# One core's fused block (attention and a mixture of experts): one routing group, token products moved between gate and up products, the last base in the late blocks, later combines in the tail

## What is computed

```
h = layernorm(x) * (1 + ca) + sa
x = x + ga * attention(h)
h = layernorm(x) * (1 + cb) + sb
aff = sigmoid(h @ wa)                       # 16 experts
topk_p, topk_i = top_k(aff, 2)              # shares, normalised to sum 1
routed = sum over the 2 chosen experts of share * w2(gelu(g(h)) * w1(h))
shared = sum over 2 shared experts of the same form, on every token
x = x + gb * (h + shared + routed)
```

## Time and profile before

| what | value |
|---|---|
| median of three executions | 1434.72 us |
| profiled execution | 1445.19 us, its span 1443.4 us |
| mean granted TensorE clock | 0.974 of full |
| busy: PE, DVE, ACT, POOL | 95%, 60%, 47%, 27% of the span |
| stage after attention | from 980.5 us to the end |

### The profile page before, as it was taken

One profiled execution on the slowest core, in us unless ns is written; L12 is line 12 of the kernel. 1 busy time (PEld: TensorE's weight loads), 2 busy tenths in 40 slices (PEclk: granted clock), 3 DMA queues, 4 the chain that ended last, 5 costly groups with the idle time before them and its releaser, 6 DMA issues. The chain is left out here.

```text
span 1443.4 us, 23277 instructions
## 1 busy us (share of the span) xinstructions
PE 1371.2 (95%) x7104; PEld 1150.2 (80%) x7104; DVE 859.9 (60%) x1776; ACT 673.5 (47%) x1554; POOL 383.9 (27%) x345
## 2 busy tenths in 40 slices
PE   6999998999999999999999999998997999999968
PEld 3666777888888888888888888886775888878756
DVE  5787754666666665666866666556565544434366
ACT  3343426666666566665766666643221332223221
POOL 0343462000003180030910307300052322322360
PEclk9999999999999999999999999999988999999979
DMA  9999868956686688776899767947343888886481
GB/s 293 363 390 349 299 252 290 358 195 226 201 308 232 194 271 290 271 261 222 295 372 334 224 203 247 333 170 272 135 166 137 300 327 314 335 306 230 131 270 44
DMA packets 160042, 375.59 MB, mean 260 GB/s; under 512 B 23144, under 2 KB 80556, under 8 KB 147680
## 3 DMA queue, kind: packets, MB, share of 16 engines
q1 hardware_dynamic: 144432, 314.34, 62.0%
q0 software_dynamic: 15536, 60.30, 11.7%
HBM read 245.84 MB, written 128.22 MB: 259 GB/s over the span
## 5 line engine op out<-in xcount | busy, mean ns | idle before, releaser
L1155 ACT ACTIVATE a_pr<-a_pr,a_stat 128x128 f32<-128x128 f32 (+3 forms) x256 | 142.0, 556 | 114.2 <-DVE a_stat L1226 114.1
L1326 PEld LDWEIGHTS a_psY<-a_pT,a_cv 128*128 128x128 f32 x768 | 124.2, 189 | 15.7 <-issue 2.1
L1226 DVE CUSTOM_DVE_ANT_0 a_pr<-a_psS,f_mask 128x128 f32<-128x128 f32 (+3 forms) x256 | 114.6, 486 | 32.5 <-PE a_psS L1314 32.1
L1326 PE MATMUL a_psY<-a_pT,a_cv 128*128 128x512 f32 (+3 forms) x768 | 130.3, 319 | 1.9 <-DVE a_pT L1245 1.9
L1161 ACT ACTIVATE a_pr<-a_pr,a_stat 128x128 f32<-128x128 f32 (+3 forms) x256 | 122.2, 548 | 0.0
L1171 ACT ACTIVATE a_oT<-a_psY 128x512 fp32r<-128x512 f32 x64 | 38.2, 596 | 150.6 <-PE a_psY L1326 150.6
L1256 DVE TENSOR_TENSOR n_acc<-a_psZ,n_acc 128x512 f32<-128x512 f32 x125 | 86.4, 691 | 36.2 <-PE a_psZ L104 33.9
L1240 DVE TENSOR_TENSOR a_oT<-a_psY,a_oT 128x512 fp32r<-128x512 f32 x64 | 44.2, 691 | 102.6 <-ACT a_oT L1171 102.6
L102 PE MATMUL a_psX<-a_hT,a_wqk 128*128 128x512 f32 (+1 forms) x256 | 100.4, 392 | 0.6 <-DVEq L1216 0.6
L103 PE MATMUL a_psX<-a_hT,a_wqk 128*128 128x512 f32 (+1 forms) x256 | 100.4, 392 | 0.0
L104 PE MATMUL a_psX<-a_hT,a_wqk 128*128 128x512 f32 (+1 forms) x256 | 100.1, 391 | 0.0
(11 more groups left out here) (357 smaller groups left out, 3499.3 us busy)
## 6 DMA issues: line engine op xcount, KB each, us to landing
w1s_d<-a_ws SPq DMA_DIRECT2D x72, 512.0 KB, 2.9
a_wqk<-wqk_d SPq DMA_DIRECT2D x64, 512.0 KB, 4.7
a_mh<-mhl_d SPq DMA_DIRECT2D x32, 1024.0 KB
s_ring<-w1s_d SPq DMA_DIRECT2D x16, 2048.0 KB, 9.1
w2s_d<-a_ws SPq DMA_DIRECT2D x72, 256.0 KB, 3.4
qpe_d<-p_qs SPq DMA_DIRECT2D x16, 1024.0 KB, 5.1
a_rw<-in_L_ffn_rw SPq DMA_DIRECT2D x128, 128.0 KB, 3.5
a_qpe<-qpe_d SPq DMA_DIRECT2D x64, 256.0 KB, 2.7
```

Source lines behind the costliest of these rows:

```text
L1155: nc.scalar.activation(pr[i], pr[i], ACT.Exp, bias=nmax[:, i:i + 1], scale=-1.0, accum_out=rsum[:, i:i + 1]).then_inc(ex, 1)
L1226: nc.vector.tensor_tensor_reduce(out=pr[i], in0=score[i][:, 0:w], in1=mask[:, S - w:S], scale=-1.0, scalar=3e38, op0=ALU.add, op1=ALU.min, ...
L1326: m = nc.tensor.matmul(psY[:, q0:S], cv[:, j, cs], pT[:, ps, o:o + w], start=n == 0, stop=n == 11)
```

## The change

One group of tiles does the routing. The transposes of batch 3 move ahead of batch 0's second products, DVE's second modulation of h moves ahead of `times(0, 2)` for that. The token products move into `first_(1, 3)`: 2 after each of the four feature chunks of the gate products, 4 after each of the up products, and the last 8 into `first_two(1)`, between its two tiles. POOL makes 18 of the 32 marking matrices and DVE 14, each signalled by itself. `tables` moves ahead of `times(1, 2)`, `shares` into block 1. `bs` is laid over the last 8 marking matrices, is not cleared any more (the one-hot rows are zero where it is not written), and its DVE part moves behind `update(1, 0)`. `last_base` moves from blocks 0 to 3 into blocks 40 to 43, and SP's wait for it behind the load of batch 2's h. AHEAD goes from 3 to 2, and the table of combines changes. The diff, cut to its core:

```diff
-            bs = sb("s_bs", [P, 2, 2 * F], F32R, own)
+        bs = hx[:, 1, 2:TB].bitcast(F32R)
...
-        AHEAD = 3
+        AHEAD = 2
...
-        tiles_m = {LAST: [[], [0], [1, 2], [3, 4]], 2: [[14], [15], [], []]}
+        tiles_m = {LAST: [[], [], [0], [1, 2]], 2: [[11], [12], [13], [14]]}
...
                 sp.dma_start(late.rearrange("p c s n -> p (c s n)").bitcast(F32),
                              K.h2T_d.rearrange("p c s n -> p (c s n)")).then_inc(late_in, 16)
+                sp.wait_ge(base3, 1)
+                for b in range(B):
+                    sp.dma_start(gb4[:, b], K.mod_d[b:b + 1, 5 * D:6 * D].broadcast_to([P, D])).then_inc(g4_in, 16)
...
-                for b in range(LAST):
-                    spots_of(b)
+                for n in range(NP):
+                    nc.gpsimd.tensor_scalar(spots[:, n], line, low[:, n // NT, n % NT:n % NT + 1], ids[:, n % NT:n % NT + 1],
+                                            ALU.is_equal, ALU.mult).then_inc(spots_ok, 1)
...
-                act.wait_ge(bs_zero, 1)
+                act.wait_ge(taken, 1)
...
-                for i in range(5, 14):
+                for i in range(3, 11):
                     scaled(i)
...
+                N.last_modulated(dve, h3, 1, ALU.add, 4, h3_ok)
+                constants_()
                 times(0, 2)
                 y_low(0, 2)
-                N.last_modulated(dve, h3, 1, ALU.add, 4, h3_ok)
-                constants_()
+                h_low(LAST, 0)
+                h_low(LAST, 1)
+                h_low(LAST, 2)
                 times(0, 3)
+                h_low(LAST, 3)
                 y_low(0, 3)
...
                 update(0, 0)
                 update(0, 1)
+                best(m1, oh1)
+                best(m2, oh2)
                 update(0, 2)
                 update(0, 3)
-                ranked(0, early)
                 times(1, 0)
                 y_low(1, 0)
-                best(m1, oh1, 1, end_)
-                best(m2, oh2, 1, end_)
+                ranked()
+                counts()
+                blocks_of()
                 times(1, 1)
                 y_low(1, 1)
-                ranked(1, end_)
-                counts()
-                blocks_of()
-                last_spots()
+                last_spots(range(NP, 25))
+                tables()
                 times(1, 2)
                 y_low(1, 2)
-                shares()
-                tables()
+                last_spots(range(25, TOP * NT))
                 times(1, 3)
                 y_low(1, 3)
                 tokens()
-                v.memset(bs[:, :, :].bitcast(U32), 0).then_inc(bs_zero, 1)
...
-                    if t == 0:
+                    if t == 1:
                         dve.wait_ge(bs_hi, 1)
...
-                    if not past(j, u, XS):
+                    if isinstance(j, int) and j == 0 and u == 1:
+                        shares()
+                    if isinstance(j, int) and j == JL - 1:
                         if u == 0:
                             dve.wait_ge(gb_in, 16 * 3)
                             dve.wait_ge(h3_out, 16)
                         N.last_base(ch, h3, gbr, u)
...
-                for i in (5, 6, 7):
+                for i in range(3, TB + TB):
                     combine([i])
                 combine([8], True)
+                finish([8])
                 combine([9], True)
-                finish([8, 9])
+                finish([9])
                 combine([10], True)
                 finish([10])
-                combine([11], True)
-                finish([11])
-                combine([12, 13], True)
                 for m in range(NU):
                     times(2, m)
                     y_low(2, m)
                     combine(tiles_m[2][m], True)
+                    if m == 0:
+                        finish([11])
+                combine([15], True)
...
                 first_(0, 2, 1, up)
+                pe.wait_ge(h3_ok, 1)
+                x_trans(LAST, 0)
                 by_token(0)
                 router(1)
+                x_trans(LAST, 1)
                 first_(0, 3, 0, gate)
                 by_token(1)
                 router(2)
+                x_trans(LAST, 2)
                 first_(0, 3, 1, up)
+                x_trans(LAST, 3)
                 first_two(0, lambda: by_token(2))
-                pe.wait_ge(h3_ok, 1)
-                x_trans(LAST, 0)
-                order(0, early)
+                router(LAST)
                 second(0, 2)
-                x_trans(LAST, 1)
+                by_token(LAST)
                 second(0, 3)
-                x_trans(LAST, 2)
                 first_(1, 0, 0, gate)
-                x_trans(LAST, 3)
+                order()
                 first_(1, 0, 1, up)
...
+                        if o < NP:
+                            pe.wait_ge(spots_ok, o + 1)
+                        else:
+                            pe.wait_ge(last_ok, o - NP + 1)
...
+                first_(1, NU - 1, 0, gate, lambda c: take(2))
+                first_(1, NU - 1, 1, up, lambda c: take(4))
+
+                def last_takes():
+                    take(8)
+                    taking[1].then_inc(taken, 1)
...
+                first_two(1, last_takes)
```

More of the change, by code:

```diff
@@ L1387, in stage_ffn @@
     NK = NBLK + 1
+    NP = 18
     JL = NBLK // XS
@@ L1734, in _ @@
                 logits(0)
+                h_high(LAST, 0)
                 y_high(0, 2)
                 logits(1)
+                h_high(LAST, 1)
                 gelu(0, 3)
                 logits(2)
+                h_high(LAST, 2)
+                h_high(LAST, 3)
                 y_high(0, 3)
-                affinity(0, early)
-                for c in range(DC):
-                    h_high(LAST, c)
-                gelu(1, 0)
                 logits(LAST)
-                y_high(1, 0)
-                affinity(1, end_)
-                for m in range(1, NU):
+                affinity()
+                for m in range(NU):
                     gelu(1, m)
@@ L1901, in tokens, with tables @@
                     v.tensor_copy(token[:, :], pl[:, 0:NK]).then_inc(token_ok, 1)
[L1903 to L1909 removed]
+                def tables():
                     ch.after(v.tensor_copy(lead[:, :], first[:, :]))
@@ L2121, in by_token, with first_ @@
                     m.then_inc(lg_t, 1)
-                def first_(b, m, a, done):
+                def first_(b, m, a, done, between=None):
                     n = place_of[b] * NU + m
@@ L2137, in first_ @@
                         r = nc.tensor.matmul(pg[:, m % 2, a], w1[:, e, c, 1, o], h[:, c, 0], start=False, stop=c == DC - 1)
+                        if between is not None:
+                            between(c)
                     r.then_inc(done, 1)
@@ L2247, in _ @@
                 first_(1, 0, 1, up)
[L2248 to L2255 removed]
+                for m in range(1, NU - 1):
                     first_(1, m, 0, gate)
                     first_(1, m, 1, up)
[L2259 to L2270 removed]
+                taking = [0, None]
@@ new lines, in take @@
+                def take(n):
+                    for _ in range(n):
+                        o = taking[0]
+                        if o % NT == 0:
+                            pe.wait_ge(takes_ok, o // NT + 1)
+                        if o < NP:
+                            pe.wait_ge(spots_ok, o + 1)
+                        else:
+                            pe.wait_ge(last_ok, o - NP + 1)
+                        taking[1] = nc.tensor.matmul(pl[:, 0:NK], spots[:, o], takes[:, o], start=o == 0, stop=o == TOP * NT - 1)
+                        taking[0] += 1
```

151 lines of the change are left out of this document (46 added, 105 removed).

## The result

| what | before | changed |
|---|---|---|
| median of four executions (lowest to highest) | 1434.55 us (1433.55 to 1438.87) | 1422.47 us (1421.50 to 1426.09) |
| profiled execution, its span | 1445.19, 1443.4 us | 1421.54, 1419.7 us |
| transposes of block 1's product | 1108.40 | 1097.98 |
| transposes of the last block's rows | 1340.98 | 1328.97 |
| from there to the end ("the tail") | 102.4 us | 90.7 us |

The ratio is 0.9915, with a 95% interval of 0.9887 to 0.9942: 12 us, or 0.85%, faster. The forecast was 1410, 24.6 us faster, so about half of it came. Against the *profiled* execution of before, though, the changed kernel's profiled execution is 23.7 us shorter, and the forecast sum was 25. Both facts need an explanation.

What follows compares the result with a forecast made beforehand. It took TensorE's waits and half clock on either side of the blocks as the bound. Front 18 plus tail 7 is 25 us, taken from 1434.7 for 1410 us, range 1398 to 1424.

Steps and rivals of the forecast that it cites:

- the front's 18 us: Routing through block 1 and just behind: block 1's transposes 17.9 us earlier, 2.1 after them, less 2 for slow clock.
- the tail's 7 us: Behind the last block: 3.5 + 2.5 - 0.5 - 1.5 + 3 = 7 us gained.
- The base and its wait: Ahead of block 1's transposes: moving `last_base` late removes PE's 5.9 us wait and slow clock; base's share 8 us.
- Bounds: 0 and 10 us of extra time. I take 2: Token products among batch 1's up products: the slow clock still costs 2 us, in a shorter stretch.
- Products 16 and 17 wait for its last matrices, 2 us in all: Batch 1's up products catch up with POOL's marking matrices; PE waits 2 us, bounds 0 and 5.
- I take 0.3: Gathers of rows ahead of block 1: PE waits 0.3 us for their landing, bounds 0 and 4 us.
- the half clock through the token products: Rival: TensorE's clock stays down through the token products, costing 8 us more, 1418 us; chance 0.18.
- The load chain: Blocks: SP's expert loads start earlier, cost 0. Rival: they do not, front's gain is lost, 1428 us; chance 0.04.
- The 3 us for unnamed waits: Tail: fewer gathers in flight shrink DVE's 5.6 and ACT's 3.8 us unnamed waits by 3 us, bounds 0 and 9.
- the 2.5 us for `times(LAST, 3)`: Tail: one combine less ahead lets it start between 1.8 and 4.5 us earlier; 2.5 us in the sum.
- unmoved unnamed waits: Rival in the tail: DVE's 5.6 and ACT's 3.8 us stay whole, tail gives 4 us, 1413 us; no separate chance given.
- The layout: Rival in the front: gathers or bias rows still wait for the token list, only the base's 8 us, 1420; chance 0.05.

Runs made afterwards that it cites:

- experiment 3: The kernel before with only `last_base` moved into blocks 40 to 43, its gate rows loaded behind it: 1426.6 us, ratio 0.992.
- experiment 1: The changed kernel with the old tail (AHEAD = 3 and the table of combines of before): 1423.8 us, ratio 0.9913.
- experiment 4: The changed kernel with `last_base` moved back into blocks 0 to 3: 1431.3 us, ratio 0.9968.
- experiment 7: The changed kernel with POOL making 12 marking matrices instead of 18 and `tables` moved behind `y_low(1, 3)`: 1416.6 us, ratio 0.9801.
- experiment 16: The changed kernel with POOL making 12 marking matrices, `tables` behind `y_low(1, 3)` and expert 1's w1 load issued later: 1413.4 us, ratio 0.9841.
- experiment 9: The kernel before, unchanged, run and profiled again on another chip: 1441.9 us, ratio 1.0008.
- experiment 10: The kernel before with AHEAD = 2 and nothing else: 1436.9 us, ratio 0.9988.
- experiment 14: The changed kernel with AHEAD = 4 and nothing else: 1422.5 us, ratio 0.9911.
- experiment 2: The kernel before with only the new tail (AHEAD = 2 and the new table of combines): 1433.4 us, ratio 0.9976.
- experiment 11: The changed kernel with the old tail (AHEAD = 3, old table of combines), run again on another chip: 1431.1 us, ratio 0.9943.
- experiment 12: The changed kernel, unchanged, run again on another chip: 1422.8 us, ratio 0.9883.
- experiment 13: The changed kernel with AHEAD = 3 and nothing else: 1422.0 us, ratio 0.9907.
- experiment 5: The changed kernel with POOL making 12 marking matrices instead of 18 and DVE 20: 1420.5 us, ratio 0.9817.
- experiment 6: The changed kernel with `tables` moved from ahead of `times(1, 2)` to behind `y_low(1, 3)`: 1424.1 us, ratio 0.9847.

## Why the prediction was right or wrong

Two steps failed: the front's 18 us, of which some 10.5 came, and the tail's 7 us, carried unchanged from the profiled execution to the median, where some 2 came.

**The base and its wait: right.** Block 1's 5.9 us wait and the slow clock behind it, 8 us of the 18, came as worked out; put in alone it gave 8.8 us (experiment 3), and taken out it left the kernel 7.5 us above experiment 1 on the same chip, which has the old tail besides (experiment 4). Of the ends forecast in the routing several were within a microsecond or so: the 0.4 us wait for the ranks (0.40), POOL's start (1051.3, measured 1050.3), the last matrix (1066.8, measured 1067.9; as this execution was 1.5 us ahead at 1004, the last is really 2.6 us late). PE does not wait for the bias rows.

**The routing and its token products: the term that was mis-sized.** Block 1's transposes were forecast at 1090.5 and stand at 1097.98, though this execution was 1.5 us ahead at 1004, before the two lists part. The front and the blocks gave 12.0 us instead of 18, and 10.5 without that head start. The parts of the shortfall:
- "Bounds: 0 and 10 us of extra time. I take 2": the slow clock cost about 4.5 us, by the busy time in it. The reason given, that 512-column products follow at once, held for its end and not for its start. I charged the waits for POOL as lost time only; the half clock came with them too, for with 1.0 us of waits instead of 2.7 it is 1.00 throughout (experiments 7 and 16). The 12.7 us at half clock from which I started were no fixed cost of the kernel before either: in experiments 9 and 10 its token products run at full clock.
- "Products 16 and 17 wait for its last matrices, 2 us in all": 2.7 us in six pieces, since a matrix took 0.98 us and not 0.86. The upper bound had the reason in it ("1.1 us beside a busier DVE").
- "I take 0.3" for the gathers: 1.3 and 1.1 us. The bounds were 0 and 4, and I took the end at which nothing happens, although I had named the three MB of weights in flight. That the load is what made the gather late is not shown, for other executions of this front have waits for rows from 0 to 1.6 us. The 1.1 us may hold the 0.7 us of turn-around at `update(1, 0)` that the sum had: in experiments 4 and 14, without a wait for rows, PE waits 0.7 us there for DVE.
These make 5.3 us, or 4.6 without that 0.7; some 2 more between the prediction's walk and the trace are small and not taken apart. Seen from the rival list, the half clock through the token products (1418, chance 0.18) was the nearer case, but half of its reason was wrong: experiment 7 has the same small products at full clock. Of the signs named for being wrong one appeared, a wait for gathered rows.

**The blocks: right to a microsecond, in the sum.** The load chain moved with block 2 (SP's wait fell from 18.0 to 10.8 us) and the later base cost nothing that PE saw. The waits for two experts grew by 2.3 us; the half clock behind such a wait, some 4 us of it from 1287 on in the kernel before, fell away.

**The tail: 7 us, and the step from the profile to the median, which is where it failed.** One combine and one finish less ahead of `times(2, 0)` is 3.5 us; PE's wait there fell from 9.5 to 10.6 us (experiments 3, 1 and 9) to 6.4 to 7.6, and the tail from 94.0 to 97.2 us without a stall to 90.7 to 93.0: right. The other terms are read from `times(LAST, 3)` and `times(2, 0)` in the changed kernel and then in experiment 1, the same front with the old tail and no stall:

```profile
1363.94 0.75 DVE L1817 SCALAR_TENSOR_TENSOR s_y<-s_pg,s_bT,s_y 128x512 f32<-128x512 f32 x1 [1.17 <-PE s_pg L2124]
...
1391.31 0.75 DVE L1817 SCALAR_TENSOR_TENSOR s_y<-s_pg,s_bT,s_y 128x512 f32<-128x512 f32 x1
...
1363.18 0.74 DVE L1816 SCALAR_TENSOR_TENSOR s_y<-s_pg,s_bT,s_y 128x512 f32<-128x512 f32 x1
...
1393.64 0.74 DVE L1816 SCALAR_TENSOR_TENSOR s_y<-s_pg,s_bT,s_y 128x512 f32<-128x512 f32 x1
```

Counted from the last block's rows, `times(LAST, 3)` starts 35.0 us on instead of 35.4: 0.4 us earlier, where I took 2.5, since with the combine gone DVE waits 1.2 us for PE's product. From there to `times(2, 0)` it is 27.4 us instead of 30.5, 3.1 less, and from there to the end 28.4 instead of 28.2. So without the stall the tail is 3.3 us shorter, and not 7. In the profiled executions the whole tail gave 11.7 us, because the stall of before was absent after. But "I take the gain over unchanged" assumed that the executions of the median had the stall too. The profiled execution was 10.5 us above that median, and the text said so; the likely meaning is that its unnamed waits were mostly not in the other executions. Of the timed ones no trace exists; experiments 1, 3 and 9 show what the old tail does without the stall. On the chips of the record and of experiments 1 to 4 the new tail is worth some 1 to 3 us: 1.3 from experiment 1 to the changed kernel, across chips, and 2.0 in experiment 2. On the chip of experiments 11 and 12 it is worth 8. The 3 us for unnamed waits, and what the 2.5 us for `times(LAST, 3)` took from ACT's late gelu (3.8 us for no named cause), should have been struck from a gain over the median. With 2 us for the tail instead of 7, and 10.5 for the front instead of 18, the sum is 12.5 and not 25; 12.1 was measured. That they agree so well is partly luck, as the front's figure comes from one execution of each kernel; by the medians experiment 1 has 11.7 us for the front on its chip and experiment 11 10.7 on its own.

**Against unmoved unnamed waits.** The Trainium skill's "Runtime: NRT & Kernel Launch", "Instruction fetch mechanics", has instructions come by a DMA queue of each engine, ahead of use; I read from it that nothing would be bought with AHEAD. In time the runs agree where they changed AHEAD alone: experiments 10, 13 and 14 show no gain or loss clear of their spread. About the fetch itself they show little. In the stall PE issues one product in 0.7 to 2.8 us with the DMA engines at 0.5 to 1.03. Between 1383 and 1406 the trace has a single packet of an instruction queue, at 1387.1, which took 0.3 us, and none from 1390 to 1404, so there is no sign of a delayed fetch. No run here changed the number of instructions or their place alone, and the cause of the stall stays open.

**The other rivals.** The layout and the load chain did what the change says, the gathers did not set the tail (PE's largest wait there is for DVE, although POOL waits 10 us for landings in the changed kernel), and 1422.5 lies inside the range, 1.5 us from its upper end.

## What to carry to other kernels

Before a profiled execution's gaps are put into a forecast, hold its time against the median: a gap without a releaser, in an execution that is 10 us above the others, is first suspected of being what makes it 10 us longer. A second profile of the kernel before would have shown it here, and in the front too. Where one engine makes small inputs for another one by one, count the waits for them twice, for the time and for TensorE's clock behind them, and give the slower producer fewer until the waits are short; here two edits that did little or nothing alone gave some 6 us together. A transfer that is issued just when megabytes of weights go out is not priced at its median: here it took 5.5 to 7.7 us instead of 3.7.

## What was not expected of the hardware

- With all token products in place, the granted clock was 1.00 throughout when PE's waits for matrices among them were two, 1.0 us in sum, and 0.50 for about 10 us when there were six of 0.36 to 0.52. Behind the gathered rows no such line can be drawn: 1.6 and 1.1 us of waiting brought it down in three profiles and 0.9 and 1.1 in one, while 0.9 to 1.3 and 1.1 us left it at 1.00 in three others.
- POOL's 128 x 128 comparison took 0.86 us each with DVE busy 75% of the time, 0.98 with 87% and 1.05 with 92% (experiment 5), but 0.93 with 68% (experiment 6): DVE's busy share alone does not give it.
- PE can issue products 0.7 to 2.8 us apart for 12 us with no wait that the trace names, while gathers keep the DMA engines busy. It happened in some profiles and not in others of one program (before and experiment 9; experiments 11 and 1). The kernel before spread over 5.4 us on one chip and 20.8 on another, the changed one over at most 8.4 on any; whether the stall makes that spread is not shown. Its cause stays open.
